# A decoder layer on one core: the third running sums ahead of the turned quotients, and the third projection's copies ahead of the turned norm's copy

## What is computed

```python
x = x + attn(layernorm(x))
x = x + xattn(layernorm(x), ctx)      # autocorrelation attention, circular shifts
x = x + ffn(layernorm(x))             # 8 experts, 2 for each row
...
# attn: 16 heads of width 8, along 64 positions of each of 128 sequences
q = feature_map(x @ wq + bq)          # x > 0: x + 1, else exp(x)
k = feature_map(x @ wk + bk)
v = x @ wv + bv
S = S + outer(k_t, v_t);  z = z + k_t
out_t = (q_t S) / (q_t z + eps);  attn = out @ wo + bo
```

## Time and profile before

| | |
|---|---|
| Runs | 625.7, 626.19, 626.98 us; median 626.19 |
| Profiled execution | 626.37 us |
| Its span in the profile | 624.5 us |
| Attention pipeline in the span | about 9 to 268 us |
| Granted clock of TensorE, mean | 0.975 |
| Busy: TensorE, VectorE, ScalarE, GpSimd | 555.4, 503.7, 394.4, 410.0 us |

### The profile page before, as it was taken

How to read it: one execution, slowest core, us unless ns; L and a number is a source line. 1 busy time by engine, 2 the same in 40 slices (tenths; PEclk the granted TensorE clock), 3 DMA queues, 4 the chain that set the end, 5 groups by cost and what they waited for, 6 DMA issues and landing times.

```text
span 624.5 us, 16196 instructions
## 1 busy us (share of the span) xinstructions
PE 555.4 (89%) x4286; PEld 409.8 (66%) x4287; DVE 503.7 (81%) x1416; ACT 394.4 (63%) x1070; POOL 410.0 (66%) x475
## 2 busy tenths in 40 slices
PE   3888999999999997978899867899999999999993
PEld 1334444444444443545788634799999999989993
DVE  4499899999999999774568888476887878877883
ACT  3455777777766764431887512445888888878882
POOL 2899888888888887111877501764576776757762
PEclk9998999999999999889999888999999999999997
DMA  5510111111161111372577470221112111111110
GB/s 153 185 52 1 35 35 35 35 34 34 34 101 42 52 43 35 64 131 65 149 206 201 79 132 14 57 50 42 32 50 53 46 48 46 52 41 50 52 45 23
DMA packets 49976, 41.03 MB, mean 66 GB/s; under 512 B 21971, under 2 KB 40278, under 8 KB 49926
## 3 DMA queue, kind: packets, MB, share of 16 engines
q1 hardware_dynamic: 44150, 29.68, 19.6%
q0 software_dynamic: 4960, 10.49, 6.5%
q10 hardware_dynamic: 816, 0.26, 0.2%
HBM read 27.54 MB, written 12.88 MB: 65 GB/s over the span
## 4 chain that ended last, share of the span: by engine, by line
PE 54%; issue 18%; DVE 15%; POOL 4%; ACT 3%; DMA 3%; DVEq 1%; SPq 1%; POOLq 0%; ACTq 0%
PE bank L1350 27%; PE run L1350 22%; DVE R L907 3%; PE bank L1354 2%; ACT xs L787 2%; PE run L1617 2%; DVE st L883 2%; POOL qk L560 1%; DVE on L962 1%; DVE mean_early L1058 1%; PE run L1541 1%; DMA ct<-in_ctx_r 1%; DMA shared<-xs_d,row_u 1%; DVE num L917 1%; ACT xrT L773 1%
## 5 line engine op out<-in xcount | busy, mean ns | idle before, releaser
L569 POOL TENSOR_TENSOR shared<-v,qk 128x1024 f32<-128x1024 f32 x64 | 125.0, 1953 | 7.5 <-POOL qk L560 4.5
L624 POOL DMA_INDIRECT shared<-xs_d,row_u x91 | 87.8, 965 | 61.8 <-DVE row_u L1248 31.2
L631 POOL DMA_INDIRECT out_x<-shared x64 | 63.6, 994 | 47.7 <-DVE shared L1320 20.9
L907 DVE TENSOR_TENSOR R<-run,qk 128x1024 f32<-128x1024 f32 x64 | 77.8, 1215 | 17.8 <-PE run L1350 17.8
L1350 PE MATMUL bank<-wqkv,xT 128*64 128x128 f32 (+1 forms) x384 | 69.8, 350 | 10.3 <-ACT v L667 9.5
L917 DVE TENSOR_REDUCE num<-R 128x128 f32<-128x1024 f32 x64 | 77.6, 1213 | 1.5
L1350 PEld LDWEIGHTS bank<-wqkv,xT 128*64 128x64 f32 (+1 forms) x384 | 33.1, 158 | 64.7 <-issue 30.1
L1350 PE MATMUL run<-shared,tris_s 64*64 64x512 f32 x512 | 71.7, 631 | 0.0
L560 POOL TENSOR_TENSOR qk<-ex,rl 128x256 f32<-128x256 f32 x64 | 46.9, 733 | 16.4 <-ACT ex L669 16.4
L816 ACT ACTIVATE shared<-run,scale_s 128x128 f32<-128x128 f32 (+1 forms) x78 | 30.0, 385 | 40.9 <-PE run L1617 40.2
L685 ACT ACTIVATE xh<-X,nb,rs 128x128 f32 (+1 forms) x126 | 52.0, 500 | 4.4 <-POOL nb L551 4.4
(11 more groups left out here) (271 smaller groups left out, 1415.6 us busy)
## 6 DMA issues: line engine op xcount, KB each, us to landing
xs_d<-xs SPq DMA_DIRECT2D x16, 270.0 KB, 5.4
X<-in_x SPq DMA_DIRECT2D x16, 256.0 KB, 2.7
ct<-in_ctx_t SPq DMA_DIRECT2D x16, 256.0 KB, 2.9
ct<-in_ctx_r SPq DMA_DIRECT2D x16, 256.0 KB, 3.9
gram_d<-gd SPq DMA_DIRECT2D x14, 256.0 KB, 2.4
w_s<-in_w_experts SPq DMA_DIRECT2D x8, 384.0 KB, 4.0
circ<-prob_d SPq DMA_DIRECT2D x30, 64.0 KB, 2.8
shared<-xs_d,row_u POOLq DMA_INDIRECT x91, 2.6
```

The costliest lines, as they stand in the source:

```text
L569: nc.gpsimd.tensor_tensor(outer[k].rearrange("p (h e d) -> p h e d", h=H, e=D), vv.unsqueeze(3).broadcast_to([P, H, D, D]), kk.unsqueeze(2 ...
L624: nc.gpsimd.indirect_dma_start(xg[q], None, xs_d[:, :], bass.IndirectOffsetOnAxis(ap=rows, axis=0)).then_inc(xg_in[q], 16)
L631: nc.gpsimd.indirect_dma_start(out[:, :], bass.IndirectOffsetOnAxis(ap=xg[(NXI + j) % NX][:, DEST:DEST + 1].bitcast(U32), axis=0), yg[q], ...
L907: nc.vector.tensor_tensor(R[:, 0:D * E].rearrange("p (h e d) -> p h e d", h=H, e=D), run[k % 2][:].rearrange("p (h e d) -> p h e d", h=H, ...
```

## The change

Two pieces of two engines' slots change places. On TensorE, sums 2 come ahead of the turning of `on` instead of behind it. On ScalarE, the copies of projection 2 come ahead of the copy `x2T` instead of behind it. This holds in all slots. Nothing else differs, and no instruction is added or left out.

```diff
@@ ScalarE, slot
                     act.wait_ge(d_k, d[0] + 1)
                     need(act, d_gram, d[0])
                     nc.scalar.activation(k2T[:], bank[4][:], ACT.Identity, bias=wkk[:, E:E + 1]).then_inc(d_kT, 1)
+                if a1:
+                    a_evac_proj(*a1, 2)
+                if d:
                     act.wait_ge(d_tr, d[0] + 1)
                     nc.scalar.activation(x2T[:], bank[5][:], ACT.Copy).then_inc(d_xT, 1)
-                if a1:
-                    a_evac_proj(*a1, 2)
                 if b:
                     denominators(*b)
@@ TensorE, slot
                 if i is None and n == NG:
                     pe.wait_ge(b_mul, NT)
                     keep_warm(2, 10)
+                if b:
+                    running_sums(*b, 2)
                 if c:
                     if a1:
                         pe.wait_ge(a_xT, a1[0] + 1)
                     pe.wait_ge(c_on, c[0] + 1)
                     transposes(bank[5], on).then_inc(c_tr, 1)
                 if i is None and n == NG:
                     keep_warm(2, 2)
-                if b:
-                    running_sums(*b, 2)
                 if d:
                     g, p, r = d
```

## The result

The changed kernel takes **620.04 us** (median of 4 runs, 617.43 to 620.77); the kernel before, in 4 runs, 626.59 (625.70 to 628.50). The ratio is 0.9884, with a 95% interval of 0.9846 to 0.9922: faster by about 1.2%, where 618.7 us (613.8 to 623.4) was forecast. Its profiled execution took 620.77 us, the longest of the four; its span is 619.0. Of the runs of the kernel before that were made beside the experiments, one of 1070.36 us was a slow run, and the ratios leave it out.

The account below looks back on a forecast made before the run. Attention slots were bound by a loop from `on` through the turn, sums 2, key projection, ScalarE copies and GpSimd to `df`. Gains of 1.9 + 1.7 + 0.2 + 1.0 + 2.9 = 7.7 us off 626.37 gave 618.7 us (613.8 to 623.4).

Parts of the forecast that it names:

- The loop: Eight rolled attention slots: key projection 0.22 us earlier, `df` waiting out GpSimd's add for tile 3; 14.61 us slots, 1.9 us gained.
- The first rival: Loop slots: `df` slips in ahead of GpSimd's add for tile 3; slots of 14.07 us, 614.4 us in all; chance 0.25.
- Group 2: Straight-line slot: sums 2 fill half of TensorE's idle time before the turn, resting on the clock holding; 1.7 us gained.
- Groups 3, 12, 13 and 14: Slots outside the loop: 0.1 us each in 3 and 12, 0.5 us each in 13 and 14, halves taken as estimates.
- Group 15: Last attention group: with the clock held, VectorE's waits for sums and for bank 6 all go; 2.9 us gained.
- The fall-back value: Group 15 if the clock falls: the wait for sums 2 still goes, plus 0.8 of the rest; 1.7 us gained.
- Behind attention ... shift whole: Means, probabilities and cross stage after attention hang on the last `df` and only move earlier with it, nothing in them touched.
- The weak case: Clock falls in groups 2 and 15 and the loop gives nothing; 3.1 us gained, 623.3 us; chance 0.13.
- It changes nothing: Key projection is tied to `zq`, the wait only gets another name, GpSimd holds the last slots; 626 us; chance 0.07.
- The slower one: Loop: GpSimd's product for tile 3 gets in ahead of `df`; slots of 15.89 us, 628.9 us in all; chance 0.05.
- evac 3's place on ScalarE forbids it: Loop: GpSimd's add for tile 3 cannot come the needed 0.9 us earlier, because of ScalarE's PSUM copies of tile 3.

Follow-up runs that it names:

- experiment 4: Changed kernel with `df` and `mv` each made by a reduction reading one SBUF input instead of two; 614.82 us, ratio 0.9790.
- experiment 1: TensorE's half of the change alone, ScalarE keeping the order of the kernel before; 620.04 us, ratio 0.9897.
- experiment 5: Changed kernel with eight spare matmuls on TensorE between sums 2 and the turn of `on` in group 15; 620.61 us, ratio 0.9894.
- experiment 6: Changed kernel with three spare statistics instructions (0.2 us each) on VectorE ahead of `df`; 632.57 us in one run.
- experiment 2: ScalarE's half of the change alone, TensorE keeping the order of the kernel before; 627.36 us, ratio 1.0010.
- experiment 7: Changed kernel with six spare statistics instructions (1.17 us) on VectorE ahead of `df`; 654.99 us in one run.
- experiment 8: Kernel before, in its old order, with `df` and `mv` made by reductions reading one SBUF input; 620.84 us, ratio 0.9902.
- experiment 9: TensorE's half of the change alone, with `df` and `mv` made by reductions reading one SBUF input; 616.05 us, ratio 0.9834.
- experiment 10: Changed kernel with one-input `df` and `mv` and eight spare TensorE matmuls in group 15; 613.06 us, ratio 0.9790.

## Why the prediction was right, and where its terms were off

**The loop, 1.9 us forecast, 3.05 measured.** The mechanism is the one written down: K starts behind `zq`, VectorE no longer waits for sums 3, and `df` stands behind features 3. Two terms of the chain were each too long by a little. `zq` ends at 158.39 and K starts at 158.44, 0.05 us, where I had 0.13 from `on`; features 3 start 7.63 us after K (166.07) against 7.70, so that the product follows at K + 8.39 (166.83) against 8.46. Together that is 0.15 us a slot, 14.45 instead of 14.61 (the last 0.01 is rounding); the alternate slot, 14.55, is still under it. The old pair of slots averages 14.885, too, where the term used 14.85 from the one shown in the earlier trace rows. Eight times (0.35 + 0.03) is the 3.05: the term was mis-sized, about half of it by taking a hand-off from another instruction.

**The first rival, `df` ahead of features 3.** It had a quarter of the chance on a margin I had at 0.05 us. In the trace features 3 start 0.12 us ahead of `df` (166.07, 166.19), and `df` takes 0.63 or 0.64 us in all eight loop slots. The forecast took the right side of a margin that its sum could not resolve, so that the loop came out on that side was in part luck. Experiment 4 gives the price: 0.42 us a slot, against the 0.54 I had. The rule of the Trainium skill that the prediction weighed ("SBUF — State Buffer", Who interferes with whom) is borne out wherever one of the two is ahead: `df` takes 0.63 behind features 3, 0.72 behind outer 2, 1.65 and 1.83 behind outer 3, and 0.16 or 0.17 in every loop slot once it reads one SBUF operand.

**Group 2, 1.7 forecast, 1.84 measured.** All steps are there: K at 57.26 (57.39 forecast), the product with sums 3 at 62.01 (62.1), a granted clock of 1.00, which is the 2.4 GHz level, where the earlier trace rows had 0.61. TensorE's timeline, then VectorE's:

```profile
55.93 0.63 PE L1355 MATMUL bank<-id_s,on 128*128 128x128 f32 x4 [1.51 <-DVE on L963]
57.26 1.10 PE L1351 MATMUL bank<-ct,wkk 128*128 128x512 f32 x2 [0.70 <-issue]
```

```profile
62.01 1.22 DVE L908 TENSOR_TENSOR R<-run,qk 128x1024 f32<-128x1024 f32 x1 [0.15 <-PE run L1351]
```

**Groups 3, 12, 13 and 14, 1.2 forecast, 1.35 measured.** The halves I took were fair together but not one by one: group 13 gave 0.32 and group 14 0.75. In group 13 `df` comes 0.06 us behind features 3 and takes 0.69 us:

```profile
223.64 0.73 POOL L560 TENSOR_TENSOR qk<-ex,rl 128x256 f32<-128x256 f32 x1 [0.41 <-ACT ex L669]
223.70 0.69 DVE L892 TENSOR_TENSOR df<-st 128x4 f32<-128x4 f32 x1
```

In group 14 it takes 0.24. With one-input `df` (experiment 4) the two slots are 13.71 and 13.74 us, so the wait at `df` is the difference between them.

**Group 15, 2.9 forecast, 2.20 measured.** This is the step that failed: "with sums 2 already made, and the clock held, all three waits go". Two of the three went, for sums 2 and for bank 6. The third, VectorE's for sums 3, stayed as it was the earlier trace rows; its row in VectorE's timeline of the changed kernel:

```profile
248.97 1.22 DVE L908 TENSOR_TENSOR R<-run,qk 128x1024 f32<-128x1024 f32 x1 [0.87 <-PE run L1351]
```

The idle time before the turn, for which the prediction had 1.9 us, is 2.29, since TensorE is done with the key sums 0.56 us earlier against VectorE's landmark than before (1.29 and 1.85 us behind it). The granted clock fell behind it to 0.74 in the stretch; the projection with `ct` at 243.50 takes 1.99 us, where 1.10 is seen at 2.4 GHz. The prediction had called the trace silent between 0.85 us of idle time, with the clock up, and 2.84. It was not: in group 2 of the kernel before, the turn follows 2.13 us of idle time, and behind it the clock is low.

```profile
56.02 0.63 PE L1354 MATMUL bank<-id_s,on 128*128 128x128 f32 x4 [2.13 <-DVE on L962]
```

Nor would its own 1.9 us have been safe: in experiment 1 group 15 has 1.82 us there, the clock reads 0.74 and the group takes 13.89 us. Experiment 5 shows that it is the clock: with the gap filled the product with sums 3 starts without a wait, and the same stretch of slot 15 is another 1.0 us shorter, 3.2 in all against the kernel before, near the 2.9 of the clock held. The fall-back value, 1.7 us, was 0.5 too low, because the wait for bank 6 went although the clock fell.

**"Behind attention ... shift whole", 0 forecast, 2.5 us lost in the profiled execution.** The last `df` is 8.52 us earlier, the first add to `X` in the cross stage 8.37, the last 5.86, the end 5.5. In the profiled execution it is what separates 620.77 from the 618.7 of the forecast; that it does so in the other runs is not shown. It was there in both profiles of the changed kernel and in that of experiment 6 (62.13 us, clock 0.97), and in none of those of the kernel before and of experiments 1, 2, 4, 7, 8, 9 and 10 (59.3 to 59.7 us); experiment 5 has 60.68 us, with a wait of 1.2 us for the same transfer. Whether the changed kernel meets it oftener than the others, as two profiles of two suggest, or whether its runs are only spread by it (617.43 to 620.77), these runs don't settle; why the transfer is late is open, and I did not try to keep TensorE busy at that place. So the total lies as near to the forecast as it does partly because errors cancelled: 1.15 us too little for the loop, 0.7 too much for group 15, and 2.5 of a loss that the sum had at nothing.

**The other rivals.** The weak case was half wrong in each part: the loop did give, and the clock held in group 2 and fell in group 15. "It changes nothing" had named the right new wait, `zq` with 0.66 us, but K moved all the same. The slower one, outer 3 ahead of `df`, did not happen in the changed kernel. Its price was near: a slot of 15.89 us was worked out, and 15.76 to 16.39 us were measured where outer 3 did come first (experiment 6, with its 0.67 us of added work in each slot). But "evac 3's place on ScalarE forbids it" was too firm. It took only 0.67 us of added VectorE work to reach it in the slots at the loop's edge, and experiment 2 met it in one slot with no work added at all.

## What to carry to other kernels

When two engines can lock each other out, the loss stands in the duration of the instruction that was kept waiting and not in any idle column: compare each cheap instruction's duration with its shortest in the trace, and see which instruction of the other engine ends with it. Before moving work around such a collision, look whether the locked-out instruction can be written with one SBUF operand: here that was worth as much as the reordering (0.9902 against 0.9884), and the two together nearly add (0.9790). An exchange that seems idle by itself, like ScalarE's half, can be the one that the next step needs, so test the halves again after every bound that is removed.

## What the runs showed of the hardware

- **Equal starts.** When `df` and a GpSimd instruction start at the same time, `df` goes through undelayed and GpSimd is stretched (0.84 for 0.73 in the earlier trace rows; 2.01 for 1.96 in experiment 2). The instruction behind `df` can then be locked out in its turn: `mv` waited 1.95 us for all of outer 3 in experiment 2, and 0.73 in slot 1 of the changed kernel. It does not have to be: beside the earlier trace rows `mv` starts at 51.14 and takes 0.17. `df` was locked out at starts 0.06 us behind GpSimd's (group 13 of the changed kernel), 0.12 (its loop) and 0.14 (outer 3 in experiment 6).
- **More work, less than its price, or more.** 0.67 us of VectorE work ahead of `df` cost 0.11 us in a loop slot; twice the work cost 2.2 us in most slots and 3.7 in two.
- **The clock and idle time.** In group 2 TensorE idled 1.51 us before the turn and 0.70 before K, and the granted clock read 1.00 behind it. In group 15 it idled 2.29 us before the turn, and the clock read 0.74. With 0.46 us left of that idle time (experiment 5) it read 1.00. In the same place 1.82 us (experiment 1) were followed by 0.74, and 1.67 us (experiment 9) by 1.00.
- **A hand-off is not one number.** From VectorE's end to TensorE's start the trace has 0.15 us for `on` (157.01 to 157.16) and 0.05 for `zq` (158.39 to 158.44), in the same slot; for `on` in group 15 it has 0.06 (242.75 to 242.81). What makes the difference is not shown.
